# Relational graph layers on one core: messages from a table of transformed nodes, or node rows gathered first and their sums transformed by groups of 27 gathers

## What is computed

```python
x0 = x
x = layernorm(x0)
for l in range(3):                                  # N = 6250 nodes, E = 200000 edges
    xr  = einsum('nd,rde->rne', x, W_rel[l])        # every node by each of 8 relations
    msg = xr[edge_type, src]                        # one row of 256 for an edge
    agg = segment_sum(msg, dst, num_segments=N)     # edges are sorted by dst
    x   = relu(agg + x @ W_root[l] + bias[l])
x1 = x0 + x
# then, on z = layernorm(x1): |z| and sign(z), two products with the
# 256 x 256 weight (its magnitudes and its signs), exp/log undone, plus bias
out = x1 + ffn(z)
```

## Time and profile before

| | us |
|---|---|
| median of 3 runs (lowest to highest) | 6615.17 (6613.16 to 6620.08) |
| span of the profiled execution | 7690.1 |
| prologue, to the first gather | 319.2 |
| first to last gather, three layers | 7324.9 |
| last gather to the end | 46.0 |

### The profile page before, as it was taken

One profiled execution on the slowest core, in us unless ns is written; L12 is line 12 of the kernel. 1 busy time (PEld: TensorE's weight loads), 2 busy tenths in 40 slices (PEclk: granted clock), 3 DMA queues, 4 the chain that ended last, 5 costly groups with the idle time before them and its releaser, 6 DMA issues.

```text
span 7690.1 us, 60783 instructions
## 1 busy us (share of the span) xinstructions
PE 4123.8 (54%) x13830; PEld 2920.8 (38%) x13831; DVE 1705.2 (22%) x3411; ACT 587.7 (8%) x1292; POOL 4737.3 (62%) x4732
## 2 busy tenths in 40 slices
PE   8755555555565555555555555554444444444444
PEld 7543444334443333333333333333333333333332
DVE  3211111111111111111111111111322223333333
ACT  4300000000000000000000000000000000000000
POOL 1266666656666646666666666665666666666665
PEclk9877777777777777777777777777767776676776
DMA  7433333333333343333333333332233333333332
GB/s 222 152 102 105 98 106 107 104 103 104 107 106 106 104 131 98 106 108 109 102 112 107 101 106 108 106 107 88 84 88 88 89 90 89 90 88 90 89 89 70
DMA packets 349844, 799.44 MB, mean 104 GB/s; under 512 B 154629, under 2 KB 180835, under 8 KB 330915
## 3 DMA queue, kind: packets, MB, share of 16 engines
q0 software_dynamic: 225776, 615.91, 27.9%
q10 hardware_dynamic: 21168, 154.15, 5.1%
q1 hardware_dynamic: 102884, 29.21, 1.6%
HBM read 638.40 MB, written 160.54 MB: 104 GB/s over the span
## 4 chain that ended last, share of the span: by engine, by line
another core or an unknown queue 39%; issue 23%; PE 22%; DVE 7%; DVEq 7%; ACT 1%; POOL 1%; ACTq 0%; DMA 0%; POOLq 0%
PE bank L465 13%; PE bank L419 3%; PE bank L449 3%; DVE acc L827 2%; DVEq L847 2%; DVE onehot L812 2%; DVEq L831 2%; PE bank L542 1%; DVEq L876 1%; POOL rows L386 1%; DVEq L840 0%; DVEq L875 0%; DVE idx_ring L859 0%; PE bank L539 0%
## 5 line engine op out<-in xcount | busy, mean ns | idle before, releaser
L386 POOL DMA_INDIRECT rows<-message_table,idx_ring x4689 | 4707.9, 1004 | 2660.4 <-issue 1528.4
L465 PE MATMUL bank<-rows,onehot 128*128 128x256 f32 x9408 | 2582.5, 434 | 2373.3 <-DVE onehot L812 1722.6
L465 PEld LDWEIGHTS bank<-rows,onehot 128*128 128x128 f32 x9408 | 2053.2, 222 | 2902.3 <-DVE onehot L812 1764.5
L827 DVE SCALAR_TENSOR_TENSOR acc<-bank,in_first,acc 128x256 f32 x588 | 283.9, 483 | 4578.9 <-remote 3649.9
L449 PE MATMUL bank<-wrel_sb,xT 128*128 128x512 f32 x1568 | 894.5, 735 | 357.8 <-ACT xT L631 220.6
L812 DVE TENSOR_TENSOR onehot<-node_iota,dst_mod 128x1024 f32<-128x1024 int16 x589 | 722.9, 1228 | 290.2 <-issue 261.1
L449 PEld LDWEIGHTS bank<-wrel_sb,xT 128*128 128x128 f32 x1568 | 363.7, 239 | 834.8 <-issue 834.5
L564 ACT COPY stage<-bank 128x512 f32<-128x512 f32 x588 | 342.4, 587 | 1366.2 <-remote 545.9
L827 DVE SCALAR_TENSOR_TENSOR acc<-bank,in_second,acc 128x256 f32 x588 | 279.4, 475 | 0.1
L859 DVE CAST idx_ring<-idx_all 128x8 uint32 x588 | 106.9, 182 | 687.4 <-issue 687.4
L626 ACT COPY xn<-acc 128x256 f32 x98 | 39.6, 404 | 2535.9 <-DVE idx_ring L859 1408.3
(11 more groups left out here) (128 smaller groups left out, 1355.5 us busy)
## 6 DMA issues: line engine op xcount, KB each, us to landing
message_table<-stage ACTq DMA_DIRECT2D x147, 1024.0 KB, 4.0
rows<-message_table,idx_ring POOLq DMA_INDIRECT x4689
wrel_sb<-in_L_gnn_W_rel_dram SPq DMA_DIRECT2D x6, 1024.0 KB, 9.8
x_sb<-in_x_dram SPq DMA_DIRECT2D x8, 768.0 KB, 14.6
x_sb<-in_x_dram SPq DMA_DIRECT2D x1, 6144.0 KB
out_dram<-x_sb SPq DMA_DIRECT2D x48, 128.0 KB
rows<-in_dst_dram POOLq DMA_DIRECT2D x1, 776.0 KB, 8.9
rows<-in_dst_dram SPq DMA_DIRECT2D x3, 196.0 KB, 7.6
```

The lines of the kernel that those rows point to most:

```text
L386: pool.indirect_dma_start(rows[:, s:s + D], None, tables[layer % 2], bass.IndirectOffsetOnAxis(ap=idx_ring[:, i, j:j + 1], axis=0),).then_ ...
L465: last = nc.tensor.matmul(seg[i % 2], onehot[:, i % 2, j, :], rows[:, s:s + D], start=(j == 0), stop=(j == CH - 1))
L827: return nc.vector.scalar_tensor_tensor(sums_of(tile), seg[buf], mask[:, ds(g, 1)], sums_of(tile), ALU.mult, ALU.add)
```

## The change

What is computed stays the same; the order of sum and relation matrix is turned round. The table of a layer (`node_table`) holds the node rows alone, 6272 rows, each as its fp32r part and its fp32r rest side by side (512 values, 2 KB). A gather brings 128 such rows. Three gathers make a triple (384 edges), nine triples a group of 27 gathers (`TPG`, 58 groups, 1566 gathers for a layer, 4698 in all).

For a triple PE multiplies the gathered rows, now the stationary operand, by a matrix of zeros and ones that has a column for each pair of relation and node place, 8 relations by a window of 16 nodes (`WIN`): 12 matmuls of 128x128 in fp32r, two halves of the features by three gathers by part and rest. DVE adds the 128x256 result to `agg` at the window's place. After nine triples PE multiplies `agg` by the 8 relation matrices (16 matmuls of 128x256 in fp32), and DVE adds that to `acc`. The root term is taken once for each tile by one of the groups: SP loads the tile's rows, PE turns them (4 matmuls in fp32r) and multiplies by the root matrix (2 in fp32). A triple that spans 16 nodes or more, or a group that spans 128 or more, would send its group through a slow path. The next table's tile is relu of the finished sums, split in two by ACT and DVE and stored.

`rows` is a ring of nine triples, 27 gathers of 2 KB rows, where it was 32 gathers of 1 KB rows. The indices, keys and places are made once in the prologue and stay in SBUF. POOL's loops are written out, so no engine fills an index ring. The prologue makes no products of nodes and relations.

```diff
-CH = 8
-RING = 4
+CH = 3
+TPG = 9
+WIN = 16
+SLOTS = P + WIN
+AHEAD = 3
...
-                        pool.wait_ge(group_done, layer * GROUPS + b * RING + (i + 1))
-                            pool.indirect_dma_start(
-                                rows[:, s:s + D], None, tables[layer % 2],
-                                bass.IndirectOffsetOnAxis(ap=idx_ring[:, i, j:j + 1], axis=0),
+                        if n >= TPG:
+                            pool.wait_ge(onehot_ready, n - TPG + 1 + AHEAD)
+                        for j in range(CH):
+                            pool.indirect_dma_start(
+                                rows[:, s:s + 2 * D].bitcast(fp32), None, tables[layer % 2],
+                                bass.IndirectOffsetOnAxis(ap=idx[:, g * TPG + k, j:j + 1], axis=0),
...
-                for j in range(CH):
-                    last = nc.tensor.matmul(seg[i % 2], onehot[:, i % 2, j, :], rows[:, s:s + D],
-                                            start=(j == 0), stop=(j == CH - 1))
+                for h in range(KH):
+                    n = 0
+                    for j in range(CH):
+                        for part in range(2):
+                            s = (k * CH + j) * 2 * D + part * D + h * P
+                            last = nc.tensor.matmul(to[:, h, :], rows[:, s:s + P], hot[:, j, :],
+                                                    start=(n == 0), stop=(n == 2 * CH - 1))
...
+                pe.wait_ge(agg_ready, gg + 1)
+                pe.wait_ge(group_done, gg + 1)
+                for r in range(R):
+                    for h in range(KH):
+                        last = nc.tensor.matmul(out_ps, agg[:, h, r, 0:P], wrel[:, h, r * D:(r + 1) * D],
+                                                start=(r == 0 and h == 0), stop=(r == R - 1 and h == KH - 1))
...
-                    add_where(i % 2, first, in_first, g)
-                    add_where(i % 2, first + 1, in_second, g).then_inc(acc_added, 1)
+                dve.wait_ge(agg_zeroed, gg + 1)
+                for k in range(TPG):
+                    dve.wait_ge(seg_ready, n + 1)
+                    dve.wait_ge(agg_added, n + 3)
+                    window = agg[:, :, :, ds(places[k], WIN)]
+                    nc.vector.tensor_tensor(window, seg[k % 3].rearrange("p h (r w) -> p h r w", r=R), window, ALU.add).then_inc(agg_added, 1)
+                    extra_tiles(layer, g, k, first, more)
+                    make_onehot(g, k + AHEAD).then_inc(onehot_ready, 1)
+                nc.vector.tensor_tensor(agg[:, :, :, 0:WIN], agg[:, :, :, 0:WIN], agg[:, :, :, P:SLOTS], ALU.add).then_inc(agg_ready, 1)
+                nc.vector.tensor_tensor(sums_of(root), root_ps, sums_of(root), ALU.add).then_inc(root_used, 1)
+                nc.vector.scalar_tensor_tensor(sums_of(first), out_ps, in_first[:, ds(g, 1)], sums_of(first), ALU.mult, ALU.add)
+                nc.vector.scalar_tensor_tensor(sums_of(first + 1), out_ps, in_second[:, ds(g, 1)], sums_of(first + 1),
+                                               ALU.mult, ALU.add).then_inc(group_done, 1)
```

More of the change, by code:

```diff
@@ L75, in gnn_ffn @@
[L75 to L83, removed]
+        wrel_at = nc.sbuf_base + (-nc.sbuf_base) % 32
@@ L441, in transform @@
[L441 to L456 removed]
+            pe.sem_inc(xT_ps_ready, 1)
@@ L583, in pair @@
-            def pair(i, ahead=None, first=False):
-                take(2 * i + 1, 1)
-                if ahead is not None:
-                    chunk_deviations(ahead)
-                store(2 * i, 2 * i, 0, 0, None if first else 16 * i)
-                take(2 * i + 2, 0)
-                store(2 * i + 1, 2 * i + 1, 1, 0, None if first else 16 * i)
-            act.sem_inc(root_used, 1)
-            act.sem_inc(rel_used, 4)
-            act.wait_ge(rel_loaded, 32)
-            for h in range(KH):
-                nc.scalar.copy(w_hi[:, h, :], wrel_sb[:, h, :]).then_inc(w_hi_ready, 1)
@@ L643, in _ @@
                 act.wait_ge(lns_ready, t + 1)
-                nc.scalar.activation(osgn, lns_sign_ps, ACT.Sign).then_inc(osgn_ready, 1)
+                nc.scalar.activation(osgn[:, :], lns_sign_ps, ACT.Sign).then_inc(osgn_ready, 1)
+                act.wait_ge(out_done, t + 1)
+                act.sem_inc(act_mark, 1)
+                with act.If(t < TILES - 1):
+                    row = nc.s_assert_within(t * P, 0, (TILES - 2) * P, skip_runtime_bounds_check_because="the branch is taken for the full tiles alone")
+                    act.dma_start(out[ds(row, P), :], res[:, :]).then_inc(out_stored, 16)
@@ new lines, in _ @@
+                with act.Else():
+                    act.dma_start(out[(TILES - 1) * P:N, :], res[0:LAST_ROWS, :]).then_inc(out_stored, 16)
+                act.wait_ge(out_stored, t * 16 + 16)
+                act.sem_inc(act_mark, 1)
+                with act.If(t < TILES - 2):
+                    row = nc.s_assert_within(t * P + P, P, (TILES - 2) * P, skip_runtime_bounds_check_because="the branch is taken where a full tile follows")
+                    act.dma_start(xres[:, :], x[ds(row, P), :]).then_inc(x_res_loaded, 16)
@@ new lines, in groups_of @@
+            def groups_of(layer, t):
+                start = dve.value_load(end_row[0:1, ds(t, 1)], min_val=0, max_val=GROUPS)
+                end = dve.value_load(end_row[0:1, ds(t + 1, 1)], min_val=0, max_val=GROUPS)
+                with dve.If(end > start):
+                    with dve.Fori(start, end) as g:
+                        group(layer, g)
+                return end
+            for layer in range(L - 1):
+                dve.wait_ge(acc_set, layer * TILES + 1)
+                with dve.Fori(0, TILES) as t:
+                    groups_of(layer, t)
+                    dve.wait_ge(hi_ready, t + (layer * TILES + 1))
+                    dve.sem_inc(dve_mark, 1)
+                    nc.vector.tensor_tensor(split[:, D:2 * D], fin_ps, split[:, 0:D].bitcast(fp32), ALU.subtract).then_inc(lo_ready, 1)
```

1111 lines of the change are left out of this document (565 added, 546 removed).

## The result

The changed kernel takes 6984.34 us (median of 4 runs, 6975.92 to 6986.50) against 6617.39 us before (4 runs): a ratio of 1.055, 95% interval 1.054 to 1.057. It is 5.5% slower; forecast were 6200 us and 6.3% faster. The profiled execution spans 6982.9 us, as long as the timed runs, so this time its length can be compared with them.

A forecast was written before the change was run, and what follows sets the result against it. POOL, issuing gathers without a pause, was taken to bind the kernel before and after. Prologue 135 + gathers 5873 + layer changes 60 + tail 35 + last layer 80 + misfit 14 = 6197, said 6200 us; own range 6100 to 6370, overall 6090 to 7160.

The forecast's parts named there:

- the formula for it: Whole kernel before: prologue + gathers x 1.25 us + what makes single gathers slower + two changes of layer + tail.
- the slow gathers: POOL gathers starting under DVE's L812, 1.88 us instead of 0.95, 253 us in all; taken as 0 after the change.
- the term for PE's pause: PE's sum for a group: 1.2 us waiting for the last add and the fold; PE keeps pace from clock 0.62.
- The second: TensorE's mean clock in the changed kernel: 0.75 before, claimed to be higher as PE has more to do.
- The last layer: Layer with the node block: PE expected near the edge of POOL's 40.0 us per tile; 80 us taken.
- PE binds the last layer: Rival: dear fp32r products or clock 0.65 make PE bind only the last layer; 6550 us, 6370 to 6750; chance 0.22.
- prologue: Start to first gather: 135 us, bounds 115 and 170, in place of 319.
- changes of layer: POOL's waits between layers, 68 and 50 us before: 30 us taken twice, 60 us.
- tail: End of the kernel, the chain as at a layer change plus one node block and last store: 35 us, 46 before.
- the misfit of 14: The 14 us by which the formula missed the kernel before's measured time, added to the forecast.
- The rival that PE binds every layer: TensorE falls to 0.50 between short fp32r bursts of a triple, a group takes 40.2 us; 7670 us; chance 0.17.
- the second rival: PE binds every layer, slower than before; 7670 us, chance 0.17; its sign: POOL waiting long for `onehot` in layer 0.

## Why the prediction was wrong, step by step

**Right.** That POOL bound the kernel before, and the formula for it. That a gather of 2 KB rows costs POOL no more (955 ns; 1.255 us from one to the next over two whole layers). That the slow gathers go (0 taken; the mean of 955 leaves at most 23 us). That a product of 128 columns costs 0.11 and 0.21. And PE's own work for a group, if the clock is given: 20.1 us at 1.00 forecast, 30.1 measured at a clock of 0.68, which is 29.6 by the same sum.

**The first step that failed** is the term for PE's pause: "plus 1.2 us in which PE waits for the last add and the fold". That is the wait ahead of the transform, and it is hardly there (8.8 us ahead of L453 in the whole run), as the root products stand in between. The wait behind the transform was left out: PE may be only three triples ahead, and DVE comes to the next group after two adds, at a tile's end after ACT's and its own split, and then loads 14 registers. PE's idle time measured 5.6 us for a group, 4.6 of it this wait. I had written that a group's end adds about 5 us to DVE and held it against POOL's 33.8, where it belonged into PE's sum: 30.1 + 5.6 is over 33.8, which makes 233 us in layers 0 and 1. With it the clock that PE needs is 20.1 / (33.8 - 5.6) = 0.71, and not the 0.62 that the prediction checked. Early register loads alone brought the idle time to 3.9 us and both layers to POOL's 1964.

**The second** is the clock: "it is 0.75 now and will be higher as PE has more to do". It was 0.68, 0.67 and 0.62. The pause that the first step left out lets the clock fall once in each group, and the short products don't bring it back: of 18444 that another one follows only 4627 began at 1.00, as at 2026.47 above, behind a transform. More work of this kind doesn't raise the clock. The rows of before could not show it, since the products there have 256 columns and 128-column matmuls come four at a time; the form was new and I gave it the clock of the old one.

**The last layer** was the largest miss: 80 us taken over POOL's pace, 624 measured (2581.5 against 1957.5). The rival "PE binds the last layer" had the place, but its upper end, 6750, was still without the pause at the start of a group and with a clock of 0.65, where 0.62 was measured. The node block made 322 us (6.6 us for a tile, where I had taken 9.1), nearly half of it slower products and not the block itself; PE's longer idle time at a tile's end made 185; and 117 are what layers 0 and 1 had too.

The whole gap of 784 us is, but for rounding, the sum of the terms: prologue 110 in place of 135, -25; layers 0 and 1 +233; last layer +544; changes of layer 80 in place of 60, +20; tail 61.6 in place of 35, +27 (PE works off the ring after the last gather); the misfit of 14 that I carried along, -14.

**The rival that PE binds every layer** named the right engine in all three layers, by a mechanism of which half is there. Pauses between bursts were to bring the clock down, and it does fall in a pause every time. But there is one such fall in a group and none between its triples, and with the pause left in, 256-column products had 0.88: the other half is that the short products leave the clock where the pause put it. Nor was the price right: 7670, where 6984 was measured. The Trainium skill ("TensorE: Matmul & The Clock Gate", "HAM oscillation — how this bites in real kernels") tells of kernels that start each burst throttled. That is seen behind the pause of 6.32 us (24 products in 5.35 us), but the 48 products that follow without a pause are as slow (10.44 us), and the section has nothing on those.

**The slow gathers**: the value 0 was right and half of its ground wrong. L908 was no evidence that two fp32 inputs in SBUF are harmless: the gather in the earlier trace rows had started 0.12 us ahead of it. The input in PSUM did it, worth 92 us in the kernel with the block one tile late. Giving the kernel before such an input was not tried; all eight banks of PSUM have a use there, four of them to half their width.

**What the profile after was to show:** the first gather came at 109.9 us (115 to 170 forecast), products at 0.11, but a clock above 0.62 was the wrong bound to test. "POOL waiting for `onehot` for long in layer 0" was the sign named for the second rival, and it is there (908.2 us in all).

## What to carry to other kernels

Where an engine works a few buffers ahead of another, put the other's way from one group to the next into the first one's sum, register loads included, and not only against the engine that binds; then move what doesn't need the awaited result ahead of the wait. A matmul of a form that the trace doesn't have gets neither the price nor the clock of its neighbours for free: here, once a pause had let the clock fall, short fp32r products left TensorE at 0.50 for 10 us in which it was never idle. And an event that overlaps another proves nothing until it is known which of them had started first.

## What the hardware did that I had not expected

An fp32r matmul with 128 moving columns, each with a weight load of its own, takes about as long from start to start as one with 256: 0.11 against 0.115 to 0.12 us at clock 1.00, 0.21 us both at 0.50. With the same number of matmuls and weight loads the 256-column form had a granted clock of 0.88 in layer 0, the 128-column form 0.68: every one of its 174 rises waited for the fp32 transform with 256 columns. A gather of 2 KB rows kept its 1.255 us while the DMA engines were busy to 0.76 at 223 GB/s (window of layer 0 with early loads). And register loads on DVE are no small thing: here is the one of nine places, shortest, median and longest in ns.

```profile
L802 DVEq TENSOR_LOAD <-meta_row x174: 844/870/1617, 113.8 to 6931.2; - x174
```

With five single loads of 0.30 us each and the register instructions between them it fills the 5.67 us ahead of 2036.08, in which the profile shows DVE neither busy nor waiting; what gives them away is idle time put down to "issue", the 963.7 us ahead of L816.
